# Mesh blocks of a graph network written out as straight code, with the norm beside the last product and other orders inside attention

## What is computed

```
cond = silu(emb @ f_w1 + f_b1) @ f_w2 + f_b2
for i in range(NUM_BLOCKS):                                  # 4
    y = _cond_layer_norm(x, cond, s1_w[i], s1_b[i], b1_w[i], b1_b[i])
    y = _sparse_attention(y, src, dst, wq[i], ..., wo[i], bo[i])
    x = x + y
    y = _cond_layer_norm(x, cond, s2_w[i], s2_b[i], b2_w[i], b2_b[i])
    y = jax.nn.relu(y @ m_w1[i] + m_b1[i]) @ m_w2[i] + m_b2[i]
    x = x + y
# _cond_layer_norm: xn * (1.0 + cond @ sw + sb) + (cond @ bw + bb), xn = (x - mu) * rsqrt(var + eps)
# _sparse_attention: ex = exp(scores - max of the row); out = (ex / sum of ex) @ v, per head; then @ wo + bo
```

## Time and profile before

| what | us |
|---|---|
| median of 3 runs | 2549.97 (2542.49 to 2558.23) |
| the profiled execution | 2558.69 |
| its span, first to last instruction | 2556.9 |
| mesh, from its first modulation to the router logits | 1219.34 to 2054.72 |

### The profile page before, as it was taken

One profiled execution on the slowest core, in us unless ns is written; L12 is line 12 of the kernel. 1 busy time (PEld: TensorE's weight loads), 2 busy tenths in 40 slices (PEclk: granted clock), 3 DMA queues, 4 the chain that ended last, 5 costly groups with the idle time before them and its releaser, 6 DMA issues.

```text
span 2556.9 us, 22909 instructions
## 1 busy us (share of the span) xinstructions
PE 2231.5 (87%) x7917; PEld 1261.0 (49%) x7917; DVE 1093.3 (43%) x2478; ACT 728.4 (28%) x1206; POOL 544.3 (21%) x474
## 2 busy tenths in 40 slices
PE   6799884888899798878898898899798799999998
PEld 3466553776445443444454454455355354444443
DVE  8796663895333333344362354335334430000002
ACT  1475543775221110002152042124115011111111
POOL 4677732442210100010101101100100220012201
PEclk9899886888999799988899899899899989999999
DMA  9432233311111100022001101100300057777742
GB/s 375 111 57 46 42 100 79 79 40 50 42 52 60 50 11 8 0 106 104 16 1 62 58 0 57 62 0 1 117 29 23 36 199 291 308 289 296 297 187 65
DMA packets 61468, 243.14 MB, mean 95 GB/s; under 512 B 23183, under 2 KB 25699, under 8 KB 39244
## 3 DMA queue, kind: packets, MB, share of 16 engines
q1 hardware_dynamic: 31866, 174.12, 19.3%
q0 software_dynamic: 26336, 62.19, 7.9%
q10 hardware_dynamic: 3168, 5.63, 0.6%
HBM read 209.96 MB, written 31.92 MB: 95 GB/s over the span
## 4 chain that ended last, share of the span: by engine, by line
PE 55%; DVE 16%; issue 16%; POOL 5%; ACT 5%; DMA 3%; PEldq 0%; PEld 0%; DVEq 0%; SPq 0%; POOLq 0%; ACTq 0%
PE PS L724 18%; PE PS L731 10%; PE PS L1221 6%; PE PS L1230 6%; PE PS L1259 6%; POOL pair_scores L1754 2%; DMA pair_scores<-TS,SIDX 2%; DVE ST L1893 1%; POOL pair_sums L1743 1%; PE PS L1020 1%; DVE Y L1901 1%; DVE AR L2184 1%; PE PS L1239 1%; PE PS L769 1%; DVE AR L2165 1%
## 5 line engine op out<-in xcount | busy, mean ns | idle before, releaser
L724 PE MATMUL PS<-XT,WR 128*128 128x113 f32 (+2 forms) x1264 | 364.1, 449 | 9.6 <-ACT XT L1327 7.6
L1725 POOL TENSOR_TENSOR RSTD<-VE,HALF 125x1 f32<-125x1 f32 x105 | 73.6, 701 | 1144.7 <-DVE VE L1896 1144.7
L724 PEld LDWEIGHTS PS<-XT,WR 128*128 128x128 f32 (+1 forms) x1264 | 199.9, 196 | 182.8 <-issue 180.7
L870 PE MATMUL PS<-HR,HOT 125*125 125x512 f32 x800 | 217.8, 422 | 38.0 <-DVE HOT L2041 38.0
L731 PE MATMUL PS<-WR,XT 128*125 128x512 f32 (+1 forms) x480 | 213.6, 598 | 6.5 <-ACT XT L1653 4.3
L2628 DVE TENSOR_TENSOR AR<-AR,PS 128x512 f32<-128x512 f32 (+1 forms) x44 | 30.3, 688 | 405.5 <-PE PS L1230 405.5
L724 PE MATMUL PS<-AR 125*128 125x512 f32 (+3 forms) x680 | 193.5, 439 | 9.3 <-ACT AR L1625 3.9
L870 PEld LDWEIGHTS PS<-HR,HOT 125*125 125x125 f32 x800 | 151.5, 198 | 81.2 <-DVE HOT L2041 30.2
L1918 DVE TENSOR_TENSOR AR<-PS,AR 125x512 f32<-125x512 f32 x55 | 38.0, 692 | 311.9 <-PE PS L731 311.4
L731 PE MATMUL PS<-WR,AR 128*125 128x512 f32 (+1 forms) x370 | 158.5, 580 | 9.9 <-ACT AR L1658 4.6
L724 PEld LDWEIGHTS PS<-AR 125*128 125x128 f32 (+1 forms) x680 | 106.1, 189 | 98.0 <-issue 89.1
(11 more groups left out here) (392 smaller groups left out, 3672.6 us busy)
## 6 DMA issues: line engine op xcount, KB each, us to landing
WR<-in_qkv SPq DMA_DIRECT2D x12, 1024.0 KB
WR<-in_omm SPq DMA_DIRECT2D x12, 1024.0 KB
pair_scores<-CNT SPq DMA_DIRECT2D x1, 12212.0 KB, 55.8
AR<-pair_scores SPq DMA_DIRECT2D x5, 2187.5 KB
AR<-in_x_a SPq DMA_DIRECT2D x10, 1024.0 KB, 9.3
AR<-in_x_b SPq DMA_DIRECT2D x10, 1024.0 KB, 5.1
AR<-in_x_c SPq DMA_DIRECT2D x10, 1024.0 KB, 7.1
WR<-in_x_a SPq DMA_DIRECT2D x8, 1024.0 KB, 9.0
```

What stands on the lines that cost most here:

```text
L724: last = mm(s.ap[0:parts, c0:c1], lhs(k), rhs(k)[:, c0:c1], start=(k == 0), stop=(k == terms - 1))
L870: last = mm(DIFF[m % 4], HOT[g % 2][0:P, k, tile(j)], HR[0:P, k, :, b, :], start=(k == 0 and b == 0), stop=(k == NT - 1 and b == 1))
L1725: g.tensor_tensor(RSTD[:, t:t + 1], VE[:, t:t + 1], HALF[:, :], ALU.pow)\
```

## The change

The loops are gone: each engine's list holds the four blocks one after the other (`for i in loops`, a Python range), with the counts of the semaphores written out. With it go the small copies (`carry`, L1886) that were there for the loop, and several small signalling copies. Parts of the new order:

- Modulations go ahead. ScalarE copies each modulation out of PSUM as GAIN (with 1 added) and OFFSET into the space of KT and V. The norm is two VectorE instructions: (x - mean) * GAIN, then times rstd plus OFFSET. One modulation stands before the last head's value products, two behind them, two beside the output projection; for the next block two stand before the second MLP product and three inside it.
- In both places the normed tiles 0, 1 and 2 are turned behind tiles 2, 3 and 4 of the product before. Tiles 3 and 4 are turned between parts of the first two projections, which are made for tiles 0 to 2, then 3, then 4 (`two_projections`). The other projections are 4 tiles (500 columns) and 1 tile (125), to match the bank.
- VectorE adds the second MLP product and does the statistics and the next block's norm tile by tile behind it (`followed(added, modulated_norm)`), in the last block also the adding to X and the final norm.
- Queries are scaled by a negative number, the mask has the other sign, and the running minimum is the exponential's bias directly: no negation (L2482). The probabilities aren't scaled at all: TensorE turns the tile as soon as it is counted; the reciprocals are broadcast and turned (5 transposes, `shares`), copied to SHARE by ScalarE, and VectorE multiplies the value product by them on its way into XT.
- Turning goes by row tile, not by column block, into one of two PT (the second one lies over the query and key weights). The five turnings of head h+1 stand between the five steps of head h's value products; those of head 0 between the value tiles. Value products take both N slots, no W slot.
- The weights of query, key and value are given back only after the last value product, so their next load starts there.

The core of the diff (lines marked "..." are left out):

```diff
-            with pe.Fori(0, BLOCKS) as i, n.loop(i, BLOCKS, loops, "block"):
...
+            def two_projections(turns, wa, ma, wb, mb):
+                copied(turns[1])
+                copied(turns[2])
+                a_ = fill("W")
+                part(a_, wa, ma, 0, 3)
+                turns.append(turn_tile(3))
+                b_ = fill("W")
+                part(b_, wb, mb, 0, 3)
+                turns.append(turn_tile(4))
+                copied(turns[3])
+                part(a_, wa, ma, 3, 4)
+                part(b_, wb, mb, 3, 4)
+                copied(turns[4])
+                part(a_, wa, ma, 4, NT)
+                part(b_, wb, mb, 4, NT)
...
+            def turn_probs(h, t):
+                s = fill("W")
+                pe.wait_ge(prob_ready, n.add(prob_ready))
+                for c in range(NT):
+                    last = nc.tensor.transpose(by_tile(s)[0:P, c, :], probs[:, t, tile(c)], ID[0:P, 0:P])
...
+            def values(h, moved, between):
+                main, rest = fill("N"), fill("N")
+                for turned_tile in moved:
+                    copied(turned_tile)
+                for k in range(NT):
+                    v_ = V[:, k, 128 * h:128 * (h + 1)]
+                    one = mm(main.ap[:, 0:MAIN], v_, PTH[h % 2][:, k, 0:MAIN], ...)
+                    two = mm(rest.ap[:, 0:TAIL], v_, PTH[h % 2][:, k, MAIN:N], ...)
...
+                    between(k)
...
+            for i in loops:
+                weights(1, 3)
+                two_projections(turns, wm(1, 0), 0, wm(1, 1), 0)
+                for h in range(1, HEADS3):
+                    project_tiles(wm(1, 0), h)
+                    project_tiles(wm(1, 1), h)
+                scores(0)
+                moved = []
+                for t in range(NT):
+                    project_narrow(wm(1, 2), t)
+                    if t >= 2:
+                        moved += [turn_probs(0, x) for x in {2: (0, 1), 3: (2, 3), 4: (4,)}[t]]
+                for h in range(HEADS3):
+                    following = []
+                    if h < HEADS3 - 1:
+                        scores(h + 1)
+                    shares(h)
...
+                    if h == HEADS3 - 1:
+                        pe.wait_ge(mod_split, n.add(mod_split))
+                        modulation(0)
+                    values(h, moved, lambda k: following.append(turn_probs(h + 1, k)) if h < HEADS3 - 1 else None)
+                    moved = following
+                weights_done()
+                modulation(1)
+                modulation(2)
+                weights(0, 3)
+                all_taken("N")
+                turns = []
+                for t in range(NT):
+                    project_narrow(wm(0, 0), t)
+                    if t < 2:
+                        modulation(3 + t)
+                    else:
+                        turns.append(turn_tile(t - 2))
+                two_projections(turns, wm(0, 1), 0, wm(0, 1), 1)
+                project_tiles(wm(0, 1), 2)
+                project_tiles(wm(0, 1), 3)
...
+                ahead = [(), (), (), ()] if i == BLOCKS - 1 else [(0, 1), (2, 3), (4,), ()]
...
+                for t in range(NT):
+                    s = fill("N")
+                    narrow(s, D, [(HT[:, k, tile(t)], wm(0, 2)[:, k, :]) for k in range(K4)])
+                    for x in ahead[min(t + 1, 3)]:
+                        modulation(x)
+                    if t >= 2:
+                        turns.append(turn_tile(t - 2))
+                weights_done()
+            turn_tile(3)
+            turn_tile(4)
...
+            def modulations():                                     # ScalarE
+                for t in range(NT):
+                    s = take("W")
+                    fn(GAIN[t], s.ap[0:P, 0:D], ACT.Copy, bias=1.0)
+                    fn(OFFSET[t], s.ap[0:P, D:2 * D], ACT.Copy).then_inc(s.taken, 1)
...
             def modulated_norm(t):                                 # VectorE
+                y = Y[0:P, t, :]
+                s, k, _ = psum.next("W")
+                dve.wait_ge(s.taken, k)
+                step(v.scalar_tensor_tensor(y, XL[:, t, :], MV[:, t, 0:1], GAIN[t], ALU.subtract, ALU.mult))
+                dve.wait_ge(rstd_ready, n.add(rstd_ready))
+                v.scalar_tensor_tensor(y, y, RSTD[:, t:t + 1], OFFSET[t], ALU.mult, ALU.add).then_inc(y_ready, 1)
...
+                for h in range(HEADS3):                            # VectorE, attention
+                    if h < HEADS3 - 1:
+                        minima(h + 1)
+                    share, at, _ = psum.next("W")
+                    if h < HEADS3 - 1:
+                        counted(h + 1)
+                    dve.wait_ge(share.taken, at)
+                    attention_of(h)
+                followed(added, modulated_norm)
```

More of the change, by code:

```diff
@@ L12 @@
-from contextlib import ExitStack, contextmanager
+from contextlib import ExitStack
 import numpy as np
@@ L66, in __init__ @@
     def __init__(self, engine):
-        self.engine, self.count, self.turn, self.per, self.base = engine, {}, None, {}, {}
+        self.engine, self.count = engine, {}
     def add(self, sem, n=1):
@@ L198, in next @@
         self.turn[kind] += 1
-        first = self.tally.turn is None and self.tally.count.get(s.filled.name, 0) == 0
+        first = self.tally.count.get(s.filled.name, 0) == 0
         before = None if first else self.tally.now(s.filled)
@@ new lines, in part, with project_tiles @@
+            def part(s, w, m, t0, t1):
+                for k in range(K4):
+                    last = mm(by_tile(s)[:, t0:t1, :], w[:, k, 128 * m:128 * (m + 1)],
+                              XT[:, k, P * t0:P * t1].rearrange("p (c n) -> p c n", n=P),
+                              start=(k == 0), stop=(k == K4 - 1))
+                if t1 == NT:
+                    last.then_inc(s.filled, 1)
+            def project_tiles(w, m):
+                s = fill("W")
+                part(s, w, m, 0, 4)
+                part(s, w, m, 4, NT)
@@ new lines, in _ @@
+                two_projections(turns, wm(0, 1), 0, wm(0, 1), 1)
+                project_tiles(wm(0, 1), 2)
+                project_tiles(wm(0, 1), 3)
+                if i < BLOCKS - 1:
+                    pe.wait_ge(mod_split, n.add(mod_split))
+                ahead = [(), (), (), ()] if i == BLOCKS - 1 else [(0, 1), (2, 3), (4,), ()]
+                hidden = [(s, n.now(s.filled)) for s in slots["W"]]
+                for x in ahead[0]:
+                    modulation(x)
+                for slot_, at in hidden:
+                    pe.wait_ge(slot_.taken, at)
@@ L1615, in round_weights, with exp_head, turned_probs @@
                 fn(MODR[:, :, :], MODW[:, j:j + 2, :], ACT.Copy).then_inc(mod_rounded, 1)
-            with act.Fori(0, BLOCKS) as i, n.loop(i, BLOCKS, loops, "block"):
-                round_weights(0, modw_in)
-                psum.skip(W=NT)
-                transpose_y()
+            def modulations():
[3 more added lines that the diff above has]
+                    fn(OFFSET[t], s.ap[0:P, D:2 * D], ACT.Copy).then_inc(s.taken, 1)
+            def exp_head(h):
+                probs = G if h % 2 == 0 else PRB
+                for t in range(NT):
+                    s, k, _ = psum.next("W")
+                    act.wait_ge(s.taken, k)
+                    fn(probs[:, t, :], probs[:, t, :], ACT.Exp, bias=DEN[:, h % 2, 0, t:t + 1], scale=-1.0)\
+                        .then_inc(exp_ready, 1)
+            def turned_probs(h):
+                for t in range(NT):
+                    s = take("W")
+                    fn(PTH[h % 2][:, :, tile(t)], by_tile(s)[0:P], ACT.Copy).then_inc(s.taken, 1)
+            round_weights(0, modw_in)
+            modulations()
+            transpose_y()
+            for i in loops:
                 round_weights(2, mod2_in)
@@ L1660, in _ @@
                 psum.skip(N=NT)
-                psum.align()
-            transpose_y()
+                if i < BLOCKS - 1:
+                    modulations()
+                transpose_y()
             psum.skip(N=1)
```

352 lines of the change are left out of this document (139 added, 213 removed).

## The result

The changed kernel takes 2428.97 us, median of 4 runs (2428.61 to 2431.82); the kernel before, on the same chip, 2548.3 (2542.49 to 2558.23). The ratio is 0.953, with a 95% interval of 0.951 to 0.955: 4.7% faster, 119 us. The forecast was 2451, 3.9%. In a later comparison the changed kernel gave 0.950 [0.947, 0.953]. The profiled execution took 2431.82, its span is 2430.0 us.

What follows compares the result with a forecast made beforehand. TensorE was taken as the bound, 35.7 us of each 207.8 us block being waits and half clock. Four blocks of 180.5 us plus start and end gave 736.5 us against 835.4, gain 99: 2451 us, range 2428 to 2488.

Steps and rivals of the forecast that it cites:

- (B): Per-block waits of TensorE: all 6 us are hidden or double-counted, 25 us less, 2426 us; chance 0.07.
- the block of 178 to 184 us: Sign that the forecast is right: this time between second modulations of the same kind.
- Ahead of the first query product: Mesh's start: 10.6 us from the first modulation to the first query product, plus 2.5 us for the clock.
- A block: Each of the four blocks on TensorE's queue: 180.5 us, work and kept waits together, where it took 207.8.
- The end: Mesh's end: less 4.3 us for modulations nothing follows, plus 4.9 for the logits, plus 0.8 for a last copy.
- The work, 174.4: TensorE's priced work per block in us: 172.1 before, plus 2.3 for the added `shares` transposes.
- a modulation: 0.86: TensorE's price in us for one modulation, 1361.64 - 1360.78; ten per block, 8.6 us.
- The waits, 6.15: TensorE waits kept per block in us: first projections' copies, scores, first turnings, last head, relu's slot, key copy, drains.
- (A): Attention: turnings between value steps cost what they cost in groups, up to +59 us, about 2500 us; chance 0.12.
- (D): Norms beside products: VectorE's tile takes over 3.9 us, 12 to 15 us a block not gained, 2507 us; chance 0.04.
- (C): Attention heads: clock falls to 1.2 GHz, +30 us a block, 2670 us, slower than before; chance 0.03.
- The step at which I set a rule of the Trainium skill aside: Norms: GpSimd contention would add 1.2 us a norm pair, 2463 instead of 2451; the forecast took nothing.

Runs made afterwards that it cites:

- the longer counting: Changed kernel with an unneeded 400-column VectorE multiplication and a wait for its end ahead of each of the 80 countings; 2444.23 us, ratio 0.957.

## Why the prediction was right, and where it was too careful

The direction, the mechanism and the place were right: the gain is covered waits and half clock at the norms. The number was nearly missed. 2429 is 7 us under the 2436 to 2470 to which I gave 0.74, and only 1 us above the lower end of the whole range; that it still lies inside is luck. Nor does that range take in (B), as I wrote: 2426 is under 2428. Of the signs to look for, the block of 178 to 184 us didn't come (174.1), nor a clock of 1.00 from the first query product on (0.62 in its first 4.3 us); the 7.5 us behind the second MLP product, no idle time over 1.5 us there and a clock of 1.00 inside the heads did come, and the logits came 126 us earlier and not 99.

The forecast's terms against the profile:

- *Ahead of the first query product*, 10.6 + 2.5: measured 10.2 and 1.6 more for the first block than for the second. Together 1.3 too much.
- *A block*, 180.5: measured 174.1. Four times 6.4 is 25.6 us, the whole miss.
- *The end*, 1.4 over a block's time: measured 2.7.

With 10.2 + 1.6 + 4 x 174.1 + 2.7 the sum is the 710.9 us of the mesh, so nothing else is missing. The 6.4 us a block come from two terms, about half and half:

**The work, 174.4.** TensorE is busy 171.2. The step that failed is "a modulation: 0.86". That number is the distance from a modulation to the product behind it; but the product that follows then holds only 3.03 us to the next modulation (1342.15 to 1345.18), where I charged it 3.44 as well. The pair is 3.9, so a modulation adds 0.46 there and 0.53 on average (the five around the second MLP product: 21.5 us from 1380.83 to the end of tile 2's turning behind it, less five product tiles of 3.44, three turnings of 0.43 and one wait of 0.41, is 2.6). Ten times 0.33 is 3.3 us. The distance between two starts of different kinds counts part of one into the other; only whole periods add up. The product pair (1.09), the value tile (3.44) and five transposes (0.54 here, 0.57 priced) were right.

**The waits, 6.15.** Measured 2.9 as idle time of the profile, and 3.7 if what the scores and the first turnings wait is read from the distances of starts: the copies ahead of the first projections 0.88 and 0.73 (priced 0.95 each), the last head 0.34 (0.5), the relu's slot 0.41 (0.3), the drains nothing (0.5), the scores 0.1 a head and not 0.3 (5.56 us for five score tiles of 1.09). A first turning waits 0.3 and not 0.55, since a counting takes 0.73 when nothing waits for its own result, not the 0.9 that I rounded up to from a group's mean of 806 ns:

```profile
1271.17 0.81 DVE L2519 CUSTOM_DVE_ANT_0 G<-G,CNT 125x625 f32<-125x625 f32 x1
1271.90 0.08 DVE L2519 DVE_READ_ACCUMULATOR2_ANT DEN<- 125x1 f32 x1
```

The accumulator is read 0.73 us after the counting began, and the next counting starts with that read. By the same figure VectorE had taken value tile 0 at 1275.7, 1.4 us before TensorE came to the slot's next product (a margin that I had put at 0.1). Nearly every wait was rounded up, so the errors had one sign; only the relu's slot was priced too low.

Of the rivals, (B), that all my waits vanish (2426), is nearest to the result, but by number only: of the 6 us of waits a block 3.7 stayed, and about half of the 25.6 us came from work and not from waits. (A) is refuted by the profile (no turning waits more than 0.3 us) and by the longer counting. (D) did not come: VectorE's tile beside the product took 3.2 us and stood idle 0.6 us a tile, as priced; the run with the turnings behind the products, the nearest to it, paid 6.9 us a place, 14 a block, which is within its 12 to 15. (C) did not come either: the clock was 1.00 through all heads. The Trainium skill, "TensorE: Matmul & The Clock Gate", section "A second HAM failure mode: psum-queue depth-cycling", tells of a kernel in which short idles between matmul groups that cycle through PSUM banks made it swing; no run here showed that, with some 40 changes between transposes and products a block and waits of 0.2 to 0.9 us between them. Where it did fall to 0.50, TensorE had been busy 5.2 of the 10 us ahead.

The step at which I set a rule of the Trainium skill aside failed in its reason. The Trainium skill, "GPSIMD Engine Reference", section "Key points", has GpSimd contend with VectorE instructions of two SBUF inputs. I took nothing because GpSimd's additions stand behind its five inverse roots. They do, but the fifth root is done before VectorE norms tile 4, and an addition waits only for its own tile: so the additions began beside the last norm pair, in each of the seven norms beside a product. The rule held, in its place: 0.74 and 0.75 us became 1.75 and 1.64, 1.9 us more for a pair where I had 1.2. In these seven norms its price was still near nothing, since tile 4 is turned last, behind a projection that covers it (1366.36 + 1.64 ends at 1368.0, the turning starts at 1368.14). At the mesh's first norm it wasn't: no product covers the norm there, the five roots were done before it began, and the run with the additions held back shows 1.8 us for two slowed instructions on TensorE's path and 1.6 for the low clock behind them (this part may be the moved modulation's too). In the two kernels with the turnings or the norms behind the product that cover is gone, and the norm instructions that GpSimd slows show in TensorE's longest waits (2.72 for tile 4 in the one, 1.71 for tile 2 in the other).

What stays open: the 124.5 us can't be split into exact parts. Undone one at a time from the changed kernel, the parts cost 52 (the turned tiles, the mesh's first start included), 24 (modulations and norms beside the second MLP product) and 8 us (turnings between the value products), and straight code alone brought 17; these overlap, and the modulations around attention, the copies that went from ScalarE and the negation of the maxima were not tried alone. Nor is it shown what made the other 8 us of straight code.

## What to carry to other kernels

Where one engine does nearly all the work and stands idle for others at a few joints, put the next stage's vector work tile by tile beside the running product, keep back small pieces of independent work (here a modulation, a turning) for the joints, and check that the helper's time for a tile is below the product's; here 3.2 us against 3.9 was enough. Price from whole periods in a running stream, not from start-to-start distances of unlike instructions, and don't round up each small wait: the two errors together hid a fifth of the gain from the forecast. A long idle stretch at a joint costs more than itself, since the clock falls behind it. Look at the first pass through a repeated stage by itself: here slowed instructions that cost next to nothing at seven places cost 1.8 us, and perhaps as much again in clock, where no product lay beside them.

## What the runs showed of the hardware

- A loop's end cost VectorE 3.3 us of "issue" (first return), and TensorE 3.3, 3.0 and 2.9 us where it waited for VectorE; the straight code had no fetch stall that shows (a block of 174.1 us with 2.9 idle).
- VectorE's instructions with two SBUF inputs of 125x512 fp32 go from 0.74 to between 1.63 and 1.77 us beside GpSimd's additions; the adding, with one input from PSUM, stays at 0.69 beside the same addition. GpSimd's addition took 1.27 beside the latter, 1.65 to 1.71 beside the slowed norm instructions of the first norm, and 1.5 as the mean of the changed kernel.
- A gap of waits is paid again in clock. After three 10 us stretches with TensorE busy 5.2 us each, the granted clock was 0.50 (1.2 GHz), 0.67 and 0.66 over the next 4 to 5 us, and eight passes took 5.34, 4.45 and 4.19 us instead of 2.76.
